# Rotary embedding: the swapped q/k halves from a second projection instead of from two copies

## The chip, the cores and the metric

The kernel runs as one program on one core of a Trainium2 chip. The metric is the device time of one launch in microseconds; lower is better. The engines are TensorE (PE in the profile, its weight loads PEld), VectorE (DVE), ScalarE (ACT), GpSimd (POOL) and SyncE (SP), which here only sends transfers.

## The reference

For x of 2 x 4096 tokens by 512 columns the kernel adds three things: x, an attention branch and an expert branch, both on the layer-normalised x. Cut to the attention's front, which the change touches:

```python
xn = layernorm(x)
c = (xn @ W_to_kv.T) @ W_compress.T              # 64 columns
ch = layernorm(c) * gamma + beta
q = ch @ W_q_comp.T
k, v = split(ch @ W_kv_comp.T)                   # 64 columns each
q = q * cos + rotate_half(q) * sin               # rotate_half(a) = concat(-a[32:], a[:32])
k = k * cos + rotate_half(k) * sin
out = x + causal_attention(q, k, v) @ ... + shared_expert(xn) + top2_of_16_experts(xn)
```

## The kernel before

Three stages follow each other: `prepare` (to about 700 us), `routed` (the 16 experts on gathered rows, to about 1500 us) and `attend`. Only `prepare` changes.

`prepare` works on 16 groups of 512 tokens. Each engine has its own program, written out by hand as functions `step(s, n, q)`: n is the group whose attention front and router are computed, s = n - 1 is the group that goes through the shared expert beside it, and q is the buffer parity. Steps 0 and 1 have their own order (`first_step`, `second_step`); 3 to 12 run in a hardware loop of pairs. Semaphores between engines are the only other thing that sets the order.

fp32 products are made of three fp32r matmuls on a high and a low part, so most tiles come as `_h` and `_l`: ScalarE writes the rounded high part, VectorE the rest. Within a step:

- TensorE computes the gate and up products of group s, the logits, transposes the compressed state (`turn_c`), does the down products, and between them the projection `qkv` (lines 439 and 440): q and k of 512 tokens, transposed, in the PSUM bank `nb`, one 128x512 output from the weights `wqk` and the state `chs`. Then it transposes the next group's normalised rows, four tiles of four transposes (`turn`, line 399), alternating between the PSUM banks `tb[1]` and `tb[0]`. Turns 2 and 3 wait for `xT_l` of the tile two before them. A wait holds up everything behind it.
- `chs` is finished by VectorE (line 721), which does `ew_l` (line 777), the low part of half an expert's weights, shortly before. `ew_l` waits for ScalarE's `ew_h` (line 546), and that for the load of these weights. The weights are sent back to memory split, for `routed`.
- The rows of `wqk` are laid out so that `nb` holds q low half, k low half, q high half, k high half (32 rows each). VectorE multiplies `nb` by the cosines into `t1` (line 746) and signals `straight`. ScalarE then copies the two 64-row halves of `nb`, swapped, into `t2` (lines 571, 572), VectorE multiplies `t2` by the sines (line 753) and adds (line 755) into `qks`. The copy of v (line 749) stands between.
- GpSimd adds the bias to x for group n (`xb`, line 996), four operations that start when VectorE has finished `h_l` of group s (line 765). SyncE's queue is in order too: the load of x for n + 2 waits for `xb`, and behind it stand the stores of the split weights, the loads of the next half expert, four stores of q and k, one of v, and the store of `base`.

Of the kernel before, what the change touches and what calls it, by code (L numbers as in the profile page):

```python
# [25 lines left out]
F32R = mybir.dt.float32r  # L26
# [11 lines left out]
R = C // 2  # L38
# [47 lines left out]
def build(nc, x, w_kv, w_compT, gamma, beta, w_qk, w_vT, w_c2l, w_outT, b_out, routerT,  # L86
# [11 lines left out]
    with ExitStack() as ctx:  # L98
# [19 lines left out]
        prepare(nc, x, w_kv, w_compT, gamma, beta, w_qk, w_vT, b_out, routerT, sh_gate, sh_up,  # L118
# [17 lines left out]
def prepare(nc, x, w_kv, w_compT, gamma, beta, w_qk, w_vT, b_out, routerT, sh_gate, sh_up,  # L136
# [3 lines left out]
    with ctx:  # L140
# [9 lines left out]
        wqk = sb("wqk", [P, 2 * C]); wqkp = [sb(f"wqk_{c}", [P, 2 * C], F32R) for c in "hl"]  # L150
# [54 lines left out]
        swap_done, straight = sem("swap_done"), sem("straight")  # L205
# [15 lines left out]
                 *((wqk[h:h + C, :], w_qk) for h in (0, C)),  # L221
# [46 lines left out]
        def _(sp):  # L268
# [71 lines left out]
            def store_qkv(n, q):  # L340
                sp.wait_ge(qk_done, n + 1)
                sp.wait_ge(v_done, n + 1)
                hold(sp, sp_gate)
                cols = slice(n * GROUP, (n + 1) * GROUP) if isinstance(n, int) else bass.ds(n * GROUP, GROUP)
                for half in range(2):
                    rows_d, at = slice(half * R, half * R + R), 2 * half * R
                    sp.dma_start(q_d[rows_d, cols], qks[q][at:at + R, :]).then_inc(st_qkv[q], 16)
                    sp.dma_start(k_d[rows_d, cols], qks[q][at + R:at + 2 * R, :]).then_inc(st_qkv[q], 16)
                vdst = v_d[n] if isinstance(n, int) else v_d[bass.ds(n, 1)].rearrange("o p c -> (o p) c")
                sp.dma_start(vdst, vs[q][:, :, :].rearrange("p j c -> p (j c)")).then_inc(st_qkv[q], 16)  # L350

            def first_expert():

                for q in range(2):
                    sp.wait_ge(st_qkv[q], 80 * NG // 2)
# [11 lines left out]
        def _(pe):  # L367
# [25 lines left out]
            def turn(n, j):  # L393
                if j == 0:
                    pe.wait_ge(xn_done, n + 1)
                if j > 1:
                    pe.wait_ge(t_ev, 4 * n + j - 1)
                for k in range(KD):
                    mm = pe.transpose(tb[1 - j % 2][:, k * P:(k + 1) * P], xn4[:, j, k * P:(k + 1) * P], ident[:, :])
                mm.then_inc(t_done, 1)  # L400
# [34 lines left out]
            def qkv(n):  # L435
                pe.wait_ge(ch_done, n + 1)
                if known(n, 0):
                    pe.wait_ge(wqk_ev, 2)
                pe.matmul(nb[:, :], wqkp[0][:, :], chs[:, :], start=True, stop=False)
                pe.matmul(nb[:, :], wqkp[1][:, :], chs[:, :], start=False, stop=True).then_inc(qkv_done, 1)  # L440
# [89 lines left out]
        def _(act):  # L530
# [36 lines left out]
            def swapped(n):  # L567

                act.wait_ge(straight, n + 1)
                after(act, qk_done, n)  # L570
                act.copy(t2[0:C, :], nb[C:P, :])
                act.copy(t2[C:P, :], nb[0:C, :]).then_inc(swap_done, 1)

# [5 lines left out]
            def first_step():  # L579
# [9 lines left out]
                swapped(0)  # L589
# [3 lines left out]
            def second_step():  # L593
# [8 lines left out]
                swapped(1)  # L602
# [3 lines left out]
            def step(s, n, q):  # L606
# [22 lines left out]
                if n is not None:  # L629
                    swapped(n)  # L630
# [7 lines left out]
        def _(dve):  # L638
# [146 lines left out]
            def first():  # L785
# [20 lines left out]
                dve.tensor_copy(wqkp[0][:, :], wqk[:, :]).then_inc(wqk_ev, 1)  # L806
                dve.wait_ge(wqk_ev, 1)
                dve.tensor_tensor(wqkp[1][:, :], wqk[:, :], value(wqkp[0][:, :]), ALU.subtract).then_inc(wqk_ev, 1)
# [60 lines left out]
            def first_step():  # L869
# [18 lines left out]
                roped_swapped(0, 0)  # L888
# [5 lines left out]
            def second_step():  # L894
# [14 lines left out]
                for j in range(GT):  # L909
# [4 lines left out]
                    if j == 0:  # L914
                        roped_swapped(1, 1)
# [3 lines left out]
            def step(s, n, q):  # L919
# [45 lines left out]
                for j in range(GT):  # L965
# [4 lines left out]
                    if j == 0 and n is not None:  # L970
                        roped_swapped(n, q)
# [787 lines left out]
def rope_tables():  # L1759
# [6 lines left out]
    cos, sin = cos.T, sin.T  # L1766
    one = np.stack([np.concatenate([cos] * 4), np.concatenate([-sin, -sin, sin, sin])], axis=1)
# [47 lines left out]
```

## Time and profile before

| | us |
|---|---|
| median of 3 runs (lowest, highest) | 1835.32 (1834.62, 1837.1) |
| profiled execution, as timed | 1835.32 |
| its span in the profile | 1833.5 |
| TensorE busy | 1755.7 |
| VectorE busy | 1130.7 |
| ScalarE busy | 771.8 |
| GpSimd busy | 662.4 |

Busy time counts instructions of an engine, not its waits. A row of a timeline gives start, length, engine, line, operation, output and inputs with their sizes, and in brackets the idle time just before and what ended it. The clock is TensorE's granted clock as a share of full speed. Buffer numbers are left out of names, so `t` is `t1` or `t2` and `tb` either bank.

### The profile page before, as it was taken

To read this page: it belongs to the slowest core of one execution; us is meant where nothing else is said; L and a number is where in the kernel's file an instruction comes from. 1 tells how busy PE (TensorE), PEld (TensorE's weight loads), DVE (VectorE), ACT (ScalarE), POOL (GpSimd) and SP (SyncE) were. 2 spreads that over 40 slices of the span, in tenths; PEclk is the share of its full clock that TensorE was granted. 3 is DMA by queue.
4 is the path that set the end of the run, shared out by engine and by line. 5 is a ranking of instruction groups with operands and counts; after the bars stand their busy time and mean duration, and the time that the engine had idled before them with its cause. 6 is when DMAs were issued, how large, how long until landed. Compare 5 with 4: busy or idle time off the path is not lost. (4 is left out here: it accounts for less than half of the span.)

```text
span 1833.5 us, 28152 instructions
## 1 busy us (share of the span) xinstructions
PE 1755.7 (96%) x8477; PEld 1402.1 (76%) x8477; DVE 1130.7 (62%) x2227; ACT 771.8 (42%) x1319; POOL 662.4 (36%) x676
## 2 busy tenths in 40 slices
PE   5699999999999998999999999999999989999998
PEld 3587778787877786778788877778888867777776
DVE  7777667777766653455555555555555436766676
ACT  3232332233222322333333344333333368888885
POOL 2544544545444442343434333433334321011110
PEclk9799999999999999999999999999999999999999
DMA  7667777766677665644544545555445438899896
GB/s 247 244 199 236 219 218 221 240 205 192 206 231 215 200 183 192 198 136 157 184 170 166 177 166 194 178 180 172 165 164 185 153 75 188 205 239 197 208 223 163
DMA packets 149934, 352.52 MB, mean 192 GB/s; under 512 B 20476, under 2 KB 41916, under 8 KB 149824
## 3 DMA queue, kind: packets, MB, share of 16 engines
q1 hardware_dynamic: 97276, 234.52, 39.5%
q0 software_dynamic: 43968, 104.91, 22.5%
q10 hardware_dynamic: 8580, 11.64, 2.3%
q8 instruction: 66, 1.08, 0.2%
q14 instruction: 44, 0.36, 0.1%
HBM read 208.24 MB, written 146.70 MB: 194 GB/s over the span
## 5 line engine op out<-in xcount | busy, mean ns | idle before, releaser
L1486 POOL DMA_INDIRECT expert_rows<-res,ids_all x143 | 150.1, 1050 | 444.8 <-ACT res L1308 435.9
L1427 DVE TENSOR_REDUCE mx<-emb 128x1 f32<-128x512 f32 (+3 forms) x288 | 175.1, 641 | 106.7 <-PE emb L1227 85.2
L70 PE MATMUL egu<-w,rT_0h 128*128 x576 | 186.9, 406 | 1.1 <-DVE rT_0l L1398 1.1
L70 PE MATMUL egu<-w,rT_1h 128*128 x568 | 182.5, 402 | 0.0
L1404 DVE TENSOR_TENSOR eh<-egu,esg 128x256 f32<-128x256 f32 x143 | 60.7, 424 | 183.6 <-ACT esg L1298 183.5
L1682 ACT ACTIVATE ex<-sc 128x1024 f32<-128x1024 f32 (+4 forms) x176 | 144.8, 823 | 55.1 <-PE sc L1627 47.3
L1034 POOL DMA_INDIRECT token_list<-tok,slot x128 | 127.1, 993 | 112.9 <-DVE slot L741 77.0
L1481 POOL DMA_INDIRECT rows<-xn_scratch,rows_all x137 | 132.9, 970 | 48.3 <-issue 43.1
L1298 ACT ACTIVATE esg<-egu 128x256 f32<-128x256 f32 x143 | 55.0, 384 | 204.7 <-PE egu L70 202.0
L1747 POOL DMA_DIRECT2D base<-expert_rows x32 | 41.3, 1527 | 264.8 <-DMA base<-base_scratch 244.2
L996 POOL TENSOR_TENSOR xb<-x,bias 128x512 f32<-128x512 f32 x64 | 88.7, 1417 | 87.9 <-DVE h_l L765 87.9
L70 PEld LDWEIGHTS egu<-w,rT_0h 128*128 128x128 f32 x576 | 104.1, 190 | 21.2 <-issue 1.9
L1626 PE MATMUL sc<-qh,khl 128*128 128x512 f32 (+3 forms) x288 | 112.2, 390 | 7.8 <-ACT pr_2h L1682 2.4
L70 PEld LDWEIGHTS egu<-w,rT_1h 128*128 128x128 f32 x568 | 101.6, 188 | 18.9 <-issue 0.4
L70 PE MATMUL egu<-w,rT_0l 128*128 x288 | 113.8, 395 | 0.0
L70 PE MATMUL egu<-w,rT_1l 128*128 x284 | 111.2, 391 | 0.0
L70 PE MATMUL gb<-wd_h,h_h 128*128 128x512 f32 x256 | 109.1, 426 | 1.1 <-DVE h_l L765 1.1
L1627 PE MATMUL sc<-qlm,kh 128*128 128x512 f32 (+3 forms) x288 | 109.0, 379 | 0.0
L1293 ACT CAST rT_0h<-etb 128x512 fp32r<-128x512 f32 x72 | 42.3, 587 | 157.6 <-PE etb L1186 142.9
L535 ACT ACTIVATE sg<-gb 128x512 f32<-128x512 f32 x64 | 38.2, 597 | 163.4 <-PE gb L70 163.4
L70 PE MATMUL gb<-wd_l,h_h 128*128 128x512 f32 x256 | 103.2, 403 | 0.0
L70 PE MATMUL gb<-wd_h,h_l 128*128 128x512 f32 x256 | 102.4, 400 | 0.0
(283 smaller groups left out, 4563.7 us busy)
## 6 DMA issues: line engine op xcount, KB each, us to landing
w<-expert_parts SPq DMA_DIRECT2D x64, 768.0 KB, 8.5
base<-expert_rows POOLq DMA_DIRECT2D x32, 1024.0 KB, 12.5
expert_parts<-ew_h SPq DMA_DIRECT2D x32, 768.0 KB
expert_parts<-ew_l SPq DMA_DIRECT2D x32, 768.0 KB
x<-x SPq DMA_DIRECT2D x16, 1024.0 KB, 6.2
xn_scratch<-xn SPq DMA_DIRECT2D x16, 1024.0 KB, 8.5
base_scratch<-xb SPq DMA_DIRECT2D x16, 1024.0 KB, 12.2
base<-base_scratch SPq DMA_DIRECT2D x16, 1024.0 KB, 6.5
```

The source lines that it names most:

```text
L70: mm = pe.matmul(dst, w, m, start=(first and i == 0), stop=(last and i == len(terms) - 1))
L996: i = pool.tensor_tensor(xb4[q][:, j, :], x4[q][:, j, :], bias[:, :], ALU.add)
L1034: pool.indirect_dma_start(list_d[:, :], bass.IndirectOffsetOnAxis(ap=slot[q][:, j, c:c + 1], axis=0), tok[q][:, j, c, :], None).then_inc(s ...
L1293: act.copy(rT[t % 2][0][:, :, :], tb[t % 2][:, :].rearrange("p (k t) -> p k t", k=KD)).then_inc(t_hi, 1)
L1298: act.activation(sg[t % 2][:, :], gu[t % 2][:, 0:FE], ACT.Silu).then_inc(sg_done, 1)
L1404: dve.tensor_tensor(h[t % 2][:, :], gu[t % 2][:, FE:2 * FE], sg[t % 2][:, :], ALU.mult).then_inc(h_done, 1)
L1427: dve.tensor_reduce(mx[n % 2][:, j, c:c + 1], mb[g % 2][:, 0:width], AX.X, ALU.max).then_inc(m_red, 1)
L1481: pool.indirect_dma_start(rows[:, t % AHEAD, :], None, xn_d[:, :], bass.IndirectOffsetOnAxis(ap=rows_all[:, t:t + 1], axis=0)).then_inc(ro ...
L1486: pool.indirect_dma_start(parts_d[:, :], bass.IndirectOffsetOnAxis(ap=ids_all[:, t:t + 1], axis=0), res[t % 2][:, :], None, bounds_check=2 ...
L1626: pe.matmul(dst, khl[:, key], qh[k % NQ][:, to:GROUP], start=True, stop=False)
L1627: mm = pe.matmul(dst, kh1[:, key], qlm[k % NQ][:, to:GROUP], start=False, stop=own < 0)
L1682: e = act.activation(dst[:, span(i)], sc[i % 2][:, span(i)], ACT.Exp, scale=SCALE)
```

## The change

A second set of weights, `w_qk_swap`, holds the same columns with the halves of each head swapped. `qkv` runs two more matmuls with it into `tb[0]`. VectorE reads the swapped values from there for the sine product, right behind the cosine product; ScalarE's copies and their two semaphores are gone. Turn 1 of the next group, the next to write `tb[0]`, waits for the sine product (`rope_done`). `qks` now holds q in its first 64 rows and k in the others, so each is one store.

```diff
-        wqk = sb("wqk", [P, 2 * C]); ...
+        wqk = sb("wqk", [P, 2, 2 * C]); ...
-                 *((wqk[h:h + C, :], w_qk) for h in (0, C)),
+                 *((wqk[h:h + C, i, :], w) for h in (0, C) for i, w in enumerate((w_qk, w_qk_swap))),
...
-                for half in range(2):
-                    rows_d, at = slice(half * R, half * R + R), 2 * half * R
-                    sp.dma_start(q_d[rows_d, cols], qks[q][at:at + R, :]).then_inc(st_qkv[q], 16)
-                    sp.dma_start(k_d[rows_d, cols], qks[q][at + R:at + 2 * R, :]).then_inc(st_qkv[q], 16)
+                sp.dma_start(q_d[:, cols], qks[q][0:C, :]).then_inc(st_qkv[q], 16)
+                sp.dma_start(k_d[:, cols], qks[q][C:2 * C, :]).then_inc(st_qkv[q], 16)
...
             def turn(n, j):
+                if j == 1:
+                    after(pe, rope_done, n)
...
-                pe.matmul(nb[:, :], wqkp[0][:, :], chs[:, :], start=True, stop=False)
-                pe.matmul(nb[:, :], wqkp[1][:, :], chs[:, :], start=False, stop=True).then_inc(qkv_done, 1)
+                for i, dst in enumerate((nb, tb[0])):
+                    pe.matmul(dst[:, :], wqkp[0][:, i, :], chs[:, :], start=True, stop=False)
+                    mm = pe.matmul(dst[:, :], wqkp[1][:, i, :], chs[:, :], start=False, stop=True)
+                mm.then_inc(qkv_done, 1)
...
-            def swapped(n):
-                act.wait_ge(straight, n + 1)
-                after(act, qk_done, n)
-                act.copy(t2[0:C, :], nb[C:P, :])
-                act.copy(t2[C:P, :], nb[0:C, :]).then_inc(swap_done, 1)
...
-                dve.tensor_tensor(t1[:, :], nb[:, :], cs[q][:, 0, :], ALU.mult).then_inc(straight, 1)
-                after(dve, st_qkv[q], times(n, q) * 5)
+                dve.tensor_tensor(t1[:, :], nb[:, :], cs[q][:, 0, :], ALU.mult)
+                dve.tensor_tensor(t2[:, :], tb[0][:, :], cs[q][:, 1, :], ALU.mult).then_inc(rope_done, 1)
+                after(dve, st_qkv[q], times(n, q) * 3)
                 dve.wait_ge(cn_done, n + 1)
                 dve.tensor_copy(vs[q][:, :, 0:C - 1], cn[:, :, 0, 0:C - 1]).then_inc(v_done, 1)
-
-            def roped_swapped(n, q):
-                dve.wait_ge(swap_done, n + 1)
-                dve.tensor_tensor(t2[:, :], t2[:, :], cs[q][:, 1, :], ALU.mult).then_inc(rope_done, 1)
                 dve.wait_ge(rope_done, n + 1)
                 dve.tensor_tensor(qks[q][:, :], t1[:, :], t2[:, :], ALU.add).then_inc(qk_done, 1)
```

On TensorE, from the projection to turn 1 of the next group, in group 2. Before:

```order
L439 MATMUL nb<-chs,wqk_h 128x512
L440 MATMUL nb<-chs,wqk_l 128x512
L70 MATMUL gb<-wd_h,h_h 128x512
L70 MATMUL gb<-wd_l,h_h 128x512
L70 MATMUL gb<-wd_h,h_l 128x512
L399 MATMUL tb<-ident,xn 128x128 x4
```

and now (line 397 is the old line 399, 69 the old 70):

```order
L438 MATMUL nb<-chs,wqk_h 128x512
L439 MATMUL nb<-chs,wqk_l 128x512
L438 MATMUL tb<-chs,wqk_h 128x512
L439 MATMUL tb<-chs,wqk_l 128x512
L69 MATMUL gb<-wd_h,h_h 128x512
L69 MATMUL gb<-wd_l,h_h 128x512
L69 MATMUL gb<-wd_h,h_l 128x512
L397 MATMUL tb<-ident,xn 128x128 x4
```

Two matmuls come in behind the two of before; all else keeps its order.

On VectorE, from the end of the projection in the loop's first group. Before:

```order
L746 TENSOR_TENSOR t_61<-nb,cs_59 128x512
L749 COPY vs<-cn 128x4x63
L772 TENSOR_TENSOR xT_0l<-tb,xT_0h 128x4x128
L783 TENSOR_TENSOR xb_0<-gb,xb_0 128x512
L753 TENSOR_TENSOR t_62<-t_62,cs_59 128x512
L755 TENSOR_TENSOR qks_63<-t_61,t_62 128x512
L772 TENSOR_TENSOR xT_0l<-tb,xT_0h 128x4x128
```

and now (758 is the old line 772, 769 the old 783):

```order
L735 TENSOR_TENSOR t_61<-nb,cs_59 128x512
L736 TENSOR_TENSOR t_62<-tb,cs_59 128x512
L739 COPY vs<-cn 128x4x63
L741 TENSOR_TENSOR qks<-t_61,t_62 128x512
L758 TENSOR_TENSOR xT_0l<-tb,xT_0h 128x4x128
L769 TENSOR_TENSOR xb_0<-gb,xb_0 128x512
L758 TENSOR_TENSOR xT_0l<-tb,xT_0h 128x4x128
```

The sine product and the sum moved ahead of the first `xT_l`. In group 0 they moved ahead of `ew_l` as well.

## Rows read from the trace of the kernel before

**Rows 1.** The page: busy us, share of the span and instructions of each engine.

```profile
PE 1755.7 (96%) x8477; PEld 1402.1 (76%) x8477; DVE 1130.7 (62%) x2227; ACT 771.8 (42%) x1319; POOL 662.4 (36%) x676
```

**Rows 2.** Stretches: length, busy us of each engine (instructions), clock, DMA share, GB/s.

```profile
60.00:700.00 640.00, 626.79 (x3023) 498.95 (x3022) 445.86 (x1074) 187.27 (x272) 305.31 (x313) 0.98 0.69 209
```

**Rows 3.** Waits, 60 to 690 us: who for whom, total us, times, longest.

```profile
ACT ew_h L546 <- DMA ew<-down_w: 33.5, 20, 3.9
...
PE nb L439 <- DVE chs L721: 8.1, 6, 3.1
```

**Rows 4.** Timeline of TensorE: the projections with the longest idle time before them.

```profile
210.32 0.50 PE L439 MATMUL nb<-chs,wqk_h 128*128 128x512 f32 x1 [1.55 <-DVE chs L721]
...
252.04 0.50 PE L439 MATMUL nb<-chs,wqk_h 128*128 128x512 f32 x1 [1.56 <-DVE chs L721]
...
534.50 0.50 PE L439 MATMUL nb<-chs,wqk_h 128*128 128x512 f32 x1 [1.07 <-DVE chs L721]
...
578.50 0.80 PE L439 MATMUL nb<-chs,wqk_h 128*128 128x512 f32 x1 [3.11 <-DVE chs L721]
```

**Rows 5.** Timeline of TensorE: a projection without a wait.

```profile
293.83 0.39 PE L439 MATMUL nb<-chs,wqk_h 128*128 128x512 f32 x1
294.06 0.39 PE L440 MATMUL nb<-chs,wqk_l 128*128 128x512 f32 x1
```

**Rows 6.** Timeline, group 1: projection, turn 1, the cosine product.

```profile
87.88 0.63 PE L440 MATMUL nb<-chs,wqk_l 128*128 128x512 f32 x1
88.31 1.06 PE L399 MATMUL tb<-ident,xn 128*128 128x128 f32 x4
...
90.44 1.05 PE L399 MATMUL tb<-ident,xn 128*128 128x128 f32 x4
...
90.50 0.68 DVE L746 TENSOR_TENSOR t<-nb,cs 128x512 f32<-128x512 f32 x1
```

**Rows 7.** Timeline of TensorE, group 10: second projection matmul, turns 1 and 2.

```profile
453.73 0.39 PE L440 MATMUL nb<-chs,wqk_l 128*128 128x512 f32 x1
...
456.05 0.60 PE L399 MATMUL tb<-ident,xn 128*128 128x128 f32 x4
...
459.29 0.60 PE L399 MATMUL tb<-ident,xn 128*128 128x128 f32 x4
```

**Rows 8.** Timeline of VectorE and GpSimd, group 10.

```profile
454.15 0.69 DVE L746 TENSOR_TENSOR t<-nb,cs 128x512 f32<-128x512 f32 x1
454.26 5.53 POOL L996 TENSOR_TENSOR xb<-x,bias 128x512 f32<-128x512 f32 x4 [5.97 <-DVE h_l L765]
454.76 0.93 DVE L749 COPY vs<-cn 128x252 f32<-128x252 f32 x1
...
458.68 1.66 DVE L755 TENSOR_TENSOR qks<-t,t 128x512 f32<-128x512 f32 x1
```

**Rows 9.** Line 755: shortest, median and longest in ns, first and last start.

```profile
L755 DVE TENSOR_TENSOR qks<-t,t x16: 691/1174/1668, 57.8 to 663.7; 128x512 f32<-128x512 f32 x16
```

**Rows 10.** Timeline of SyncE's queue, group 10: the base store.

```profile
468.04 0.39 SPq L338 DMA_DIRECT2D base_scratch<-xb  x1
```

**Rows 11.** Timeline of the start, five engines.

```profile
4.56 1.20 SPq L286 DMA_DIRECT2D wqk<-w_qk  x2
...
12.62 1.97 PE L460 MATMUL nb<-wcT,ht 128*128 128x64 f32 x8 [12.62 <-DMA token<-token_in]
...
15.98 0.23 DVE L806 CAST wqk_h<-wqk 128x128 fp32r<-128x128 f32 x1
...
55.36 1.76 DVE L777 TENSOR_TENSOR ew_l<-ew,ew_h 128x1536 fp32r<-128x1536 f32 x1 [2.60 <-ACT ew_h L546]
...
58.37 1.28 DVE L772 TENSOR_TENSOR xT_1l<-tb,xT_1h 128x512 fp32r<-128x512 f32 x2
...
59.10 1.97 PE L399 MATMUL tb<-ident,xn 128*128 128x128 f32 x8 [7.09 <-DVE xT_1l L772]
```

**Rows 12.** Stretch behind the second wait of rows 4, columns as rows 2.

```profile
253.00:256.50 3.50, 3.50 (x13) 2.78 (x13) 2.24 (x4) 1.75 (x3) 3.50 (x3) 0.52 0.00 0
```

More of the change, by code:

```diff
@@ L37 @@
 C = 64
-R = C // 2
 LAT = 128
@@ L83, in hold, with build @@
     eng.sem_inc(gate, 1)
-def build(nc, x, w_kv, w_compT, gamma, beta, w_qk, w_vT, w_c2l, w_outT, b_out, routerT,
+def build(nc, x, w_kv, w_compT, gamma, beta, w_qk, w_qk_swap, w_vT, w_c2l, w_outT, b_out, routerT,
           gate_w, up_w, down_w, sh_gate, sh_up, sh_down, rope, ident_in, tri_in, route_in, upto_in, token_in, tile_p_in, fold_in, out):
@@ L117, in build @@
         w_in, st_base, stored = sems("w_in", 2), sems("st_base", 2), sems("rstored", 2)
-        prepare(nc, x, w_kv, w_compT, gamma, beta, w_qk, w_vT, b_out, routerT, sh_gate, sh_up,
+        prepare(nc, x, w_kv, w_compT, gamma, beta, w_qk, w_qk_swap, w_vT, b_out, routerT, sh_gate, sh_up,
                 sh_down, rope, ident_in, tri_in, route_in, upto_in, token_in, tile_p_in, q_d, k_d, v_d, base_d, xn_d, list_d,
@@ L133, in build, with prepare @@
         attend(nc, q_d, max_d, base_d, parts_d, out, ident, khl, kh1, vhl, mop, queries, masks, stored, base, base_in, placed)
-def prepare(nc, x, w_kv, w_compT, gamma, beta, w_qk, w_vT, b_out, routerT, sh_gate, sh_up,
+def prepare(nc, x, w_kv, w_compT, gamma, beta, w_qk, w_qk_swap, w_vT, b_out, routerT, sh_gate, sh_up,
             sh_down, rope, ident_in, tri_in, route_in, upto_in, token_in, tile_p_in, q_d, k_d, v_d, base_d, xn_d, list_d,
@@ L149, in prepare @@
         wcT = sb("wcT", [P, C])
-        wqk = sb("wqk", [P, 2 * C]); wqkp = [sb(f"wqk_{c}", [P, 2 * C], F32R) for c in "hl"]
+        wqk = sb("wqk", [P, 2, 2 * C]); wqkp = [sb(f"wqk_{c}", [P, 2, 2 * C], F32R) for c in "hl"]
         gam = sb("gam", [P, 1]); bet = sb("bet", [P, 1]); bias = sb("bias", [P, D])
@@ L204, in prepare @@
         d_done, d_ev = sem("d_done"), sem("d_ev")
-        swap_done, straight = sem("swap_done"), sem("straight")
         scattered = [sem("scattered0"), sem("scattered1")]
@@ L354, in first_expert @@
                 for q in range(2):
-                    sp.wait_ge(st_qkv[q], 80 * NG // 2)
+                    sp.wait_ge(st_qkv[q], 48 * NG // 2)
                 sp.wait_ge(st_xn, 16 * NG)
@@ L588, in first_step @@
                 expert_high(0, 1)
-                swapped(0)
                 for j in range(GT):
@@ L601, in second_step @@
                 expert_high(1, 1)
-                swapped(1)
                 for j in range(GT):
@@ L628, in step @@
                     hidden_high(s, 3)
-                if n is not None:
-                    swapped(n)
                 if n is not None and not known(n, NG - 1):
@@ L805, in first @@
                 dve.wait_ge(wc_ev, 3)
-                dve.tensor_copy(wqkp[0][:, :], wqk[:, :]).then_inc(wqk_ev, 1)
+                dve.tensor_copy(wqkp[0][:, :, :], wqk[:, :, :]).then_inc(wqk_ev, 1)
                 dve.wait_ge(wqk_ev, 1)
-                dve.tensor_tensor(wqkp[1][:, :], wqk[:, :], value(wqkp[0][:, :]), ALU.subtract).then_inc(wqk_ev, 1)
+                dve.tensor_tensor(wqkp[1][:, :, :], wqk[:, :, :], value(wqkp[0][:, :, :]), ALU.subtract).then_inc(wqk_ev, 1)
                 for j in range(GT):
@@ L887, in first_step @@
                 expert_low(0, 1)
-                roped_swapped(0, 0)
                 for j in range(GT):
@@ L913, in second_step @@
                     turned_low(2, 0, j)
-                    if j == 0:
-                        roped_swapped(1, 1)
                     if j == 1:
@@ L969, in step @@
                         added(s, 1 - q, j)
-                    if j == 0 and n is not None:
-                        roped_swapped(n, q)
                     if j == 1 and n is not None:
@@ L1765, in rope_tables @@
     cos, sin = np.cos(angle).astype(f), np.sin(angle).astype(f)
-    cos, sin = cos.T, sin.T
-    one = np.stack([np.concatenate([cos] * 4), np.concatenate([-sin, -sin, sin, sin])], axis=1)
+    cos = np.concatenate([cos, cos], axis=1).T
+    sin = np.concatenate([-sin, sin], axis=1).T
+    one = np.stack([np.concatenate([cos, cos]), np.concatenate([sin, sin])], axis=1)
     seq = one.reshape(2 * C, 2, QB, GROUP).transpose(2, 0, 1, 3)
@@ L1794 @@
     wqT, wkT, wvT = wq.T, wkv[:C].T, wkv[C:].T
+    swap = lambda w: np.concatenate([w[:, C // 2:], w[:, :C // 2]], axis=1)
     ident, tri, route, upto, token, tile_p, fold = shape_tables()
@@ L1798 @@
         "gamma": a["L0_attn_ln_gamma"][:, None], "beta": a["L0_attn_ln_beta"][:, None],
-        "w_qk": np.concatenate([wqT[:, :R], wkT[:, :R], wqT[:, R:], wkT[:, R:]], axis=1),
+        "w_qk": np.concatenate([wqT, wkT], axis=1), "w_qk_swap": np.concatenate([swap(wqT), swap(wkT)], axis=1),
         "w_vT": wvT, "w_c2l": a["L0_attn_W_comp2lat"], "w_outT": a["L0_attn_W_out_res"].T, "b_out": a["L0_attn_b_out_res"],
```

## The prediction

> **What bounds the kernel now.** I read the busy shares first: TensorE is busy for 1755.7 of 1833.5 us [rows 1]. The table of stretches then shows where the change acts: it touches only the preparation, up to about 700 us, where TensorE is busy for 626.8 of 640 us at a clock of 0.98 [rows 2]. ScalarE has 187 us of work there and VectorE 446, so work taken from them is worth nothing by itself; work given to TensorE is paid unless it falls into a wait. The table of waits says which waits there are. Where TensorE stands idle, it is for `chs` from VectorE, just ahead of the q/k projection that the change doubles, and ScalarE spends 33.5 us waiting for expert weights to land, which stand ahead of `chs` on VectorE [rows 3]. The four longest of these idle times are 1.55, 1.56, 1.07 and 3.11 us [rows 4]. So there are two loops of about 40 us per group: TensorE's instruction stream, and expert weights to `chs`. Usually the first is the later one, in a few groups the second. From here on n is the group, 0 to 15, and every time is of one profiled execution, span 1833.5 us, 1835.32 us as timed; the 1.8 us around the span I leave as they are. That execution equals the median shown.
>
> **Two more matmuls in each group.** In a running stream the two projection matmuls start 0.23 us apart (293.83, 294.06) [rows 5]. They are 128x512 like the two that are added, so a group costs 2 x 0.23 = 0.46 us. In group 0 this costs nothing: TensorE waits for the normalised rows of the next group afterwards. Groups 2 to 15: 14 x 0.46 = 6.4 us. In group 1 TensorE runs at the lower of its two clocks, 1.2 GHz (matmul 0.63 us against 0.39, the next thing starts 0.43 us later [rows 6]), so 0.86 us.
>
> **What of that falls into waits.** In the four groups of [rows 4] `chs` comes from the weights' loop. It starts again when VectorE finishes `h_l` and GpSimd can add the bias (the `xb` operations), after which SyncE, having waited for them, sends the x load, the weight stores and the next weight loads. None of this waits for the projection. TensorE arrives 0.46 us later at the next wait, and the wait is 0.46 us shorter: -4 x 0.46 = -1.8 us. Shorter idle entries are left out. Bounds: nothing is hidden (0), or all of groups 2 to 14 (-6.0).
>
> **The new wait of turn 1.** Transposing tile 1 of the next group writes `tb[0]`, which now holds the swapped projection, so it waits until VectorE has multiplied it by the sines. Ahead of it stand, on TensorE, three matmuls, the four transposes of tile 0 and three matmuls. In group 10 the last projection matmul starts at 453.73 and turn 1 at 456.05, 2.32 us later. Its weight load stands 0.23 us before it, one matmul's pitch, so it must be released at +2.09 [rows 7]. VectorE starts the first product at 454.15 (+0.42) and, as the distance to the next row shows, takes an instruction of this kind every 0.61 us [rows 8]. The second product is new in this form (PSUM times SBUF into SBUF), but it is the form and size of the first, 0.69 us: it ends at 0.42 + 0.61 + 0.69 = +1.72. Some 0.1 us for the signal, an estimate, leaves 0.27 us of margin, 0 to 0.1 in groups where TensorE does not start from a wait. I take 0.1 us in a few groups. In group 1 there is no margin: the first product starts at 90.50, the second ends at 91.80, and turn 1, which began at 90.44, could begin at 90.44 + 0.86 = 91.30 [rows 6]. With 0.2 us for signal and weight load it waits 0.7 us. Everything behind it waits too, since TensorE is in order. If it never waited, this term is 0; if VectorE were late by a `v` copy, about 1 us.
>
> **Turn 2 and the shared port.** Turn 2 waits for `xT_l` of tile 0. VectorE now does both products, the copy of v and the sum before it, where the sine product and the sum stood behind it. Two of those, the copy and the sum, run into GpSimd's four `xb` operations. The sum takes 1.66 us in group 10, ending after GpSimd's last operation (454.26 + 5.53 = 459.79, sum 458.68 to 460.34), against 0.69 us as its shortest [rows 8, 9]. So each of the two may wait for one GpSimd operation of some 1.3 us. Shifted by the 0.46 us, GpSimd's first operation starts at about +0.07 relative to the last projection matmul. The copy asks at +1.65, is let in at +2.5 and ends at 2.8; the sum is let in at about +3.8 and ends at 4.5; `xT_l` runs to 5.1. Turn 2 begins at 459.29 - 453.73 = +5.56, its weight load at 5.33 [rows 7]. Margin 0.1 to 0.2 us. Together with turn 1 of the running groups I enter +0.3 us; the bounds are 0 and, if both lose one more operation, the first rival below. GpSimd then ends at the same time as now within 0.1 to 0.5 us, which is why I let the weights' loop stand.
>
> The Trainium skill, page "SBUF — State Buffer", section "SBUF: two separate sides", calls this an exclusive lock: a VectorE instruction with two SBUF inputs and a GpSimd operation that reads SBUF exclude each other for a whole instruction. The trace agrees (1.66 against 0.69 us). By that rule the sine product leaves the lock, since one input now comes from PSUM, and the sum stays in it, now in front of turn 2.
>
> **What goes.** Two ScalarE copies, VectorE's wait for them and the `straight` signal. Nobody on the path waits for them in running groups, since ScalarE is idle most of the time: 0. Two of five stores per group leave SyncE's queue, the bytes stay: 0, since q, k and v are not read before the preparation ends. What they free is that the base store behind them is issued earlier, 1 to 2 us before its 468.04 [rows 10].
>
> **Start.** Two more constant loads stand in SyncE's queue ahead of those that the first matmul waits for. Two such issues take 1.20 us; the first matmul waits until 12.62, and everything after it hangs on it [rows 11]: +1.2. Rounding and splitting 256 instead of 128 columns: 0.23 us for the cast at 128 columns; with a doubling at most 0.5 for the pair, I take +0.3. On the other side, VectorE now finishes its rope work in the idle time ahead of 55.36 and not between `ew_l` and `xT_l`, and ScalarE has no swap in front of its tile copies at 55.36. `xT_l` begins when `ew_l` is through (55.36 + 1.76 = 57.12) and not at 58.37, and turn 2 at 59.10 follows: -1.3 [rows 11]. Bounds of the three together: -0.5 and +2.
>
> **Sum.** 6.4 + 0.86 - 1.8 + 0.7 + 0.3 + 1.5 - 1.3 = +6.7 us. The gathers and the attention start later by that and are unchanged. Span 1840.2, time 1842.0 us.
>
> **Rivals.**
> *A. The port makes turn 2 the bound.* The copy or the sum loses one more GpSimd operation: 1.3 us less the 0.15 of margin is 1.15 us in 13 groups, 15 us: 1857. For it: the sum did lose a whole one [rows 8]. Against it: they lose one each in my count already. 8%.
> *B. The base store collides with the weights.* Issued 1.6 us earlier, it shares the transfer queues with the weight loads still under way. If half of that time is lost to the weights in ten groups, 8 us come on top: 1850. For it: ScalarE waits for just these loads [rows 3]. Against: the order in the queue is unchanged. 10%.
> *C. The weights' loop sets the pace.* Where `chs` releases TensorE everywhere, all 6.0 us of groups 2 to 14 are hidden, 4.2 more than in the sum: 1838. One wait of [rows 4] that gets shorter may also spare a fall to the lower clock: after the 1.56 us the granted clock was 0.52, the 1.2 GHz level, for 3.5 us [rows 12], which costs about half of that, 1.6 us. Then 1836. For it: idle before `chs` is seen in many groups. Against: TensorE is 98% busy. 14%.
> *D. Not slower: the weights land earlier.* Two stores fewer per group leave the queue behind the weight loads. Place: ScalarE's wait for `ew`. If they landed 1.5 us earlier, the four waits would go (7.3 us, of which 1.8 is counted) and two falls of the clock (3.2): 1842.0 - 5.5 - 3.2 = 1833.3. It decides from about 1 us of earlier landing. Against it: the stores stand behind the loads, so they can only have disturbed them by overlap. 8%.
> The Trainium skill, page "DMA: Bandwidth & Descriptors", section "Anatomy of one DMA", gives each transfer about 2 us of fixed cost whatever its size, so by that page two fewer are worth 4 us per group if somebody waits. No row here has anybody waiting for them; it speaks for D alone.
>
> **How the numbers follow.** The forecast, slower by 3 to 10 us (1838.5 to 1845), has 60%; A 8, B 10, C 14, D 8. About 0.2%, 3.7 us, is what a measurement of this kernel can tell from no change. Slower beyond it: most of the forecast (55) and A and B (18), 73%. Within: rest of the forecast, C and a little of D, 20%. Faster: 7%. The range reaches over C below and B above: 1835.5 to 1850; A and most of D stay out.
>
> **What would show it.** Two matmuls more per group into `tb`, 0.23 us apart, and TensorE's busy time up by 6 to 8 us. Idle before the projection about 0.46 us shorter in the groups of [rows 4]. Turn 1 with a wait for the sine product in group 1 and hardly elsewhere. Turn 2 without wait; if it shows one of 1 us in most groups, A is right. First matmul at about 13.8 us. If ScalarE's 33.5 us of waiting for `ew` falls or rises by more than 10 us, D or B. The forecast is wrong if the preparation doesn't end 4 to 10 us later.

## The result and the profile after

| | before, us | changed, us |
|---|---|---|
| median (lowest, highest; runs) | 1834.5 (1832.97, 1837.1; 6) | 1843.73 (1838.6, 1844.86; 6) |
| profiled execution, as timed | 1835.32 | 1834.49 |
| its span | 1833.5 | 1832.7 |

The changed kernel takes 1.0053 of the time of before, 95% interval 1.0036 to 1.0069: slower, by 9.7 us in the middle of the interval, where I had forecast 6.7. But its profiled execution was a quick one, 4 us under the fastest of its timed runs. On its trace alone the change would look free, so I use it for the order of things and compare a second trace of each kernel. These are from two other chips, on which before takes 1850.24 us (the changed kernel's) and 1850.69 us (before's); times are compared as ratios on one chip only.

The first trace of the changed kernel answers the busy times of [rows 1] and the stretch of [rows 2]:

```profile
PE 1759.1 (96%) x8509; PEld 1406.6 (77%) x8509; DVE 1135.1 (62%) x2227; ACT 752.7 (41%) x1287; POOL 660.1 (36%) x676
...
60.00:700.00 640.00, 630.54 (x3055) 503.76 (x3054) 450.34 (x1077) 169.49 (x242) 303.58 (x313) 0.99 0.68 210
```

32 more matmuls, and ScalarE has 18 us less to do there. Group 10 in its timeline, against [rows 7, 8]:

```profile
456.56 0.39 PE L439 MATMUL nb<-chs,wqk_l 128*128 128x512 f32 x1
456.79 0.39 PE L438 MATMUL tb<-chs,wqk_h 128*128 128x512 f32 x1
457.02 0.39 PE L439 MATMUL tb<-chs,wqk_l 128*128 128x512 f32 x1
457.09 5.54 POOL L977 TENSOR_TENSOR xb<-x,bias 128x512 f32<-128x512 f32 x4 [5.91 <-DVE h_l L751]
457.45 0.69 DVE L735 TENSOR_TENSOR t<-nb,cs 128x512 f32<-128x512 f32 x1 [0.56 <-PE tb L439]
...
458.06 0.68 DVE L736 TENSOR_TENSOR t<-tb,cs 128x512 f32<-128x512 f32 x1
458.66 1.13 DVE L739 COPY vs<-cn 128x252 f32<-128x252 f32 x1
459.09 0.60 PE L397 MATMUL tb<-ident,xn 128*128 128x128 f32 x4
459.71 1.77 DVE L741 TENSOR_TENSOR qks<-t,t 128x512 f32<-128x512 f32 x1
461.40 0.68 DVE L758 TENSOR_TENSOR xT_1l<-tb,xT_1h 128x512 fp32r<-128x512 f32 x1
...
462.33 0.60 PE L397 MATMUL tb<-ident,xn 128*128 128x128 f32 x4
```

The added matmuls start 0.23 us apart, turn 1 (459.09) has no bracket and so no wait, nor has turn 2 (462.33). The sum takes 1.77 us. This part went as worked out. The second trace of the changed kernel, its page and its table of waits (60 to 690 us):

```profile
span 1854.0 us, 28109 instructions
...
PE 1765.4 (95%) x8509; PEld 1408.7 (76%) x8509; DVE 1137.0 (61%) x2227; ACT 753.5 (41%) x1287; POOL 657.5 (35%) x676
...
ACT ew_h L546 <- DMA ew<-down_w: 57.5, 23, 7.3
...
PE nb L438 <- DVE chs L710: 9.5, 10, 2.4
...
PE tb L397 <- DVE t L736: 0.3, 1, 0.3
```

and the second trace of before:

```profile
span 1851.0 us, 28152 instructions
...
PE 1758.0 (95%) x8477; PEld 1402.1 (76%) x8477; DVE 1132.2 (61%) x2227; ACT 771.9 (42%) x1319; POOL 656.2 (35%) x676
...
ACT ew_h L546 <- DMA ew<-down_w: 53.0, 25, 5.6
...
PE nb L439 <- DVE chs L721: 17.8, 9, 5.2
```

TensorE is 7.4 us busier, and its idle time for `chs` is 8.3 us shorter: the matmuls stand where it would have waited. Yet the span is 3.0 us longer. Where that arises is seen at `chs` of group 2 and of group 15, changed:

```profile
127.74 0.69 DVE L710 TENSOR_TENSOR chs<-t,chs 64x512 fp32r<-64x512 f32 x1
...
674.47 0.69 DVE L710 TENSOR_TENSOR chs<-t,chs 64x512 fp32r<-64x512 f32 x1
```

and before:

```profile
128.53 0.69 DVE L721 TENSOR_TENSOR chs<-t,chs 64x512 fp32r<-64x512 f32 x1
...
672.26 0.69 DVE L721 TENSOR_TENSOR chs<-t,chs 64x512 fp32r<-64x512 f32 x1
```

In group 2 the changed kernel is 0.8 us ahead; from there to group 15 it needs 546.7 us against 543.7. A pair of traces does not prove 3 us, since executions differ by as much (the first pair has 527.9 against 530.1) and these two come from different chips; it says where to look. In the first pair TensorE's idle time for `chs` is shorter, too, against 8.1 us in [rows 3]:

```profile
PE nb L438 <- DVE chs L710: 1.0, 2, 0.6
```

### The profile page after: what moved, and what is told of

It is laid out like the page before. It is cut to its first block and busy times, and to the rows that moved or that the text cites. A ratio compares the mean times of both kernels' runs of the same rounds, so it can differ in the third digit from the quotient of the medians.

```text
span 1832.7 us, 28109 instructions
## 1 busy us (share of the span) xinstructions
PE 1759.1 (96%) x8509; PEld 1406.6 (77%) x8509; DVE 1135.1 (62%) x2227; ACT 752.7 (41%) x1287; POOL 660.1 (36%) x676
## 5 line engine op out<-in xcount | busy, mean ns | idle before, releaser
L69 PEld LDWEIGHTS egu<-w,rT_1h 128*128 128x128 f32 x568 | 101.7, 188 | 19.8 <-issue 0.6
```

Source lines behind the costliest of these rows:

```text
L69: mm = pe.matmul(dst, w, m, start=(first and i == 0), stop=(last and i == len(terms) - 1))
```

## The experiments

All ratios are against before on the same chip, with 95% intervals. The first batch asks which part of the change costs the time.

**The changed kernel again, with a second trace.** No edit.

> The changed kernel once more. Its six timed runs had a median of 1843.7 us, but the one execution that was profiled took 1834.5 us, so its trace may be an untypical one. If the extra time is TensorE's two added matmuls alone, every execution pays it and this one's preparation ends 6 us later or more; the quick execution then had luck in its waits. If the extra time comes from the loop of expert weights (weights landing later, TensorE idle before the projection), this trace shows more idle time before the projection than the quick one, and the time scatters by several us from run to run. Ratio to before: 1.004 to 1.006 by either.

Measured: 1.0036 (1.0022 to 1.0049). Slower again, on another chip; the interval overlaps the first. The trace shows more idle time before the projection than the quick one (9.5 us against 1.0) and more waiting for the weights (57.5 against 32.4), the sign that was named for the loop of weights. The kernel before shows as much of a difference between its own two traces (17.8 against 8.1, 53.0 against 33.5), so the sign does not tell the change from the chip.

**Before, with the projection done twice.** The two matmuls are issued twice into `nb`, nothing else:

```diff
-                pe.matmul(nb[:, :], wqkp[0][:, :], chs[:, :], start=True, stop=False)
-                pe.matmul(nb[:, :], wqkp[1][:, :], chs[:, :], start=False, stop=True).then_inc(qkv_done, 1)
+                for i in range(2):
+                    pe.matmul(nb[:, :], wqkp[0][:, :], chs[:, :], start=True, stop=False)
+                    mm = pe.matmul(nb[:, :], wqkp[1][:, :], chs[:, :], start=False, stop=True)
+                mm.then_inc(qkv_done, 1)
```

> The kernel of before, whose projection into nb is simply done twice with the same weights (same result): two more 128x512 matmuls per group and nothing else, no new wait, no other order on VectorE, the same stores. Theory 1, TensorE's stream pays: 14 x 0.46 us plus group 1, less what falls into waits, +4 to +7 us, ratio 1.002 to 1.004, that is most of what the change costs. Theory 2, the cost is in the weights' loop, which the other parts of the change lengthened: the doubling falls into the waits for chs, 0 to +3 us, ratio under 1.002.

Measured: 0.9993 (0.998 to 1.0005), which is -1.3 us (-3.7 to +0.9). With 32 more matmuls in the same place the kernel is not measurably slower. The largest term of my sum was 6.4 us, 4.6 after what falls into waits, and both lie outside the interval. But the doubling moves something else as well. VectorE starts on `nb` later (1.60 us after `chs`, 0.95 in the second trace of before) and its sum no longer meets GpSimd (median 0.69 us, as when free), and the x load is issued 6.21 us after `chs` instead of 6.51 (means of groups 2 to 12). So this run shows the net of the matmuls and of a slightly shorter loop of weights, not the matmuls alone. A pair without this difference comes in the third batch.

**The changed kernel with four stores of q and k again**, of 32 rows each, as before the change:

```diff
-                sp.dma_start(q_d[:, cols], qks[q][0:C, :]).then_inc(st_qkv[q], 16)
-                sp.dma_start(k_d[:, cols], qks[q][C:2 * C, :]).then_inc(st_qkv[q], 16)
+                for lo in (0, C // 2):
+                    half = slice(lo, lo + C // 2)
+                    sp.dma_start(q_d[half, cols], qks[q][half, :]).then_inc(st_qkv[q], 16)
+                    sp.dma_start(k_d[half, cols], qks[q][C + lo:C + lo + C // 2, :]).then_inc(st_qkv[q], 16)
```

> The changed kernel with q and k stored in four pieces of 32 rows again, as before, so that the base store and the rope load are issued as late as they were. Theory 1: no difference to the changed kernel, +9 us against before. Theory 2 in the form of rival B (the base store, issued earlier, disturbs the landing of the expert weights): 3 to 8 us faster than the changed kernel, and the first half of the weights lands about 11 us after the issue of its last load instead of about 12.3.

Measured: 1.0032 (1.0015 to 1.0049), as without the edit. In the trace the base store is issued 14.9 us after `chs` instead of 13.95 (means of groups 2 to 12), the first half of the weights lands 0.4 us sooner and the second 1.0 us later. The number of stores and the moment of the base store make no difference that shows.

**The changed kernel with one constant load per half**: `w_qk` and `w_qk_swap` side by side in one array, so that SyncE's queue has no more issues than before:

```diff
-                 *((wqk[h:h + C, i, :], w) for h in (0, C) for i, w in enumerate((w_qk, w_qk_swap))),
+                 *((wqk[h:h + C, :, :], w_qk.rearrange("p (i c) -> p i c", i=2)) for h in (0, C)),
```

> The changed kernel with the two sets of projection weights in one array, so that as many constant loads stand ahead of the first matmul as before. By the prediction the start gets 1.2 us shorter (first matmul at about 12.6 instead of 13.9 us) and the whole kernel 1.2 us faster than the changed one. If the start is absorbed later, no difference in time.

Measured: 1.0015 (1.0001 to 1.003). The trace has `chs` of group 2 at 126.52 instead of 127.74. The ratios differ by 3.9 us, with overlapping intervals; the trace shows 1.2 us, the two issues, and no cause for more.

What is left is the new place of the sine product, the copy of v and the sum. The second batch moves them.

**The copy of v and the sum behind the third `xT_l`**, in the changed kernel. GpSimd's `xb` operations then have the port to themselves:

```diff
                 dve.tensor_tensor(t2[:, :], tb[0][:, :], cs[q][:, 1, :], ALU.mult).then_inc(rope_done, 1)
+
+            def summed(n, q):
                 after(dve, st_qkv[q], times(n, q) * 3)
...
+                    if j == 2 and n is not None:
+                        summed(n, q)
```

> The changed kernel with the copy of v and the sum moved on VectorE from just behind the products to behind the third xT_l, when GpSimd's four xb operations have ended. Theory P: the load of x is issued 0.5 us earlier after chs (6.2 instead of 6.7), each of some 12 groups gets 0.5 us shorter, 5 to 7 us less than the changed kernel, about the time of before. Theory S: the scatters start even earlier (the sum, 1.8 us, no longer stands before them), so no gain or a loss of a few us.

Measured: 1.0076 (1.0063 to 1.0089), the opposite of what the port's theory wanted, though its first half came true. Group 6 of this kernel:

```profile
303.17 0.69 DVE L710 TENSOR_TENSOR chs<-t,chs 64x512 fp32r<-64x512 f32 x1
304.79 5.04 POOL L984 TENSOR_TENSOR xb<-x,bias 128x512 f32<-128x512 f32 x4 [6.71 <-DVE h_l L753]
310.17 0.37 SPq L274 DMA_DIRECT2D x<-x  x1
311.74 1.08 POOL L1022 DMA_INDIRECT token_list<-tok,slot  x1 [1.91 <-DVE slot L730]
313.51 0.56 SPq L302 DMA_DIRECT2D ew<-down_w  x1
326.66 1.48 ACT L546 CAST ew_h<-ew 128x1536 fp32r<-128x1536 f32 x1 [3.87 <-DMA ew<-down_w]
```

of the changed kernel:

```profile
298.45 0.69 DVE L710 TENSOR_TENSOR chs<-t,chs 64x512 fp32r<-64x512 f32 x1
300.07 5.55 POOL L977 TENSOR_TENSOR xb<-x,bias 128x512 f32<-128x512 f32 x4 [6.45 <-DVE h_l L751]
302.68 1.78 DVE L741 TENSOR_TENSOR qks<-t,t 128x512 f32<-128x512 f32 x1
304.38 0.68 DVE L758 TENSOR_TENSOR xT_1l<-tb,xT_1h 128x512 fp32r<-128x512 f32 x1
305.96 0.37 SPq L274 DMA_DIRECT2D x<-x  x1
309.15 1.08 POOL L1015 DMA_INDIRECT token_list<-tok,slot  x1 [3.53 <-DVE slot L730]
309.44 0.93 SPq L302 DMA_DIRECT2D ew<-down_w  x1
321.17 1.48 ACT L546 CAST ew_h<-ew 128x1536 fp32r<-128x1536 f32 x1 [3.09 <-DMA ew<-down_w]
```

and of before:

```profile
296.31 0.69 DVE L721 TENSOR_TENSOR chs<-t,chs 64x512 fp32r<-64x512 f32 x1
300.37 0.69 DVE L772 TENSOR_TENSOR xT_1l<-tb,xT_1h 128x512 fp32r<-128x512 f32 x1 [1.01 <-ACT xT_1h L576]
303.68 0.38 SPq L276 DMA_DIRECT2D x<-x  x1
306.86 0.50 SPq L304 DMA_DIRECT2D ew<-down_w  x1
307.52 1.08 POOL L1034 DMA_INDIRECT token_list<-tok,slot  x1 [4.06 <-DVE slot L741]
318.07 1.48 ACT L546 CAST ew_h<-ew 128x1536 fp32r<-128x1536 f32 x1 [2.32 <-DMA ew<-down_w]
```

From the end of `chs` in group 6, the x load comes at 6.31 us with the sum late, 6.82 in the changed kernel and 6.68 before. So the `xb` operations do end earlier when VectorE leaves them alone. But `token_list`, the first of GpSimd's eight small scatters, comes at 7.88, 10.01 and 10.52, and from the issue of the last weight load to `ew_h` it is 13.15, 11.73 and 11.21 us. In these three traces, the earlier the scatters, the later the weights. The scatters wait for VectorE's `slot`. Before the change VectorE stood idle for 1.01 us ahead of the first `xT_l`, because ScalarE did its swap copies before its part of that tile; in the changed kernel the rope work fills this time, so `slot` and the scatters come sooner. With the sum late, the copy of v and the sum no longer stand ahead of `slot` at all. Here is the rate of the transfers in two stretches, 12 to 14 and 14 to 16 us after `chs` (last column, GB/s; the others as in [rows 2]), with the sum late:

```profile
315.90:317.90 2.00, 2.00 (x11) 1.65 (x10) 0.00 (x0) 0.00 (x0) 1.66 (x2) 1.00 1.03 426
317.90:319.90 2.00, 2.00 (x11) 1.48 (x10) 0.00 (x0) 0.45 (x1) 1.39 (x3) 1.00 1.14 209
```

in the changed kernel, with the two microseconds after:

```profile
311.10:313.10 2.00, 2.00 (x10) 1.66 (x9) 0.00 (x0) 0.00 (x0) 1.39 (x3) 1.00 1.05 428
313.10:315.10 2.00, 2.00 (x10) 1.53 (x9) 0.00 (x0) 0.36 (x1) 1.70 (x2) 1.00 1.02 405
315.10:317.10 2.00, 2.00 (x10) 1.28 (x9) 1.04 (x2) 0.86 (x2) 1.39 (x3) 1.00 1.11 209
```

and before, 14 to 16, 16 to 18 and 18 to 20 us:

```profile
311.00:313.00 2.00, 2.00 (x10) 1.49 (x9) 0.00 (x0) 0.59 (x1) 1.39 (x3) 1.00 1.01 402
313.00:315.00 2.00, 2.00 (x10) 1.33 (x9) 1.27 (x2) 0.63 (x2) 1.63 (x2) 1.00 1.14 311
315.00:317.00 2.00, 2.00 (x11) 1.60 (x10) 2.00 (x5) 0.58 (x1) 1.45 (x2) 1.00 1.16 320
```

The DMA share stays at 1 or above while the rate falls, some 6 us after the first scatter: from 426 and 405 to 209 GB/s in the first two kernels, from 402 to 311 before. One would guess that the scatters occupy the transfer engines. The queues say otherwise. With the sum late, the same two stretches by queue (packets, MB, share of the time of 16 engines; q1 holds SyncE's transfers, q0 GpSimd's scatters), first 315.9 to 317.9:

```profile
q1 hardware_dynamic: 159, 0.85, 101.7%
q0 software_dynamic: 32, 0.00, 1.2%
```

and 317.9 to 319.9:

```profile
q1 hardware_dynamic: 68, 0.42, 112.7%
q0 software_dynamic: 27, 0.00, 1.6%
```

The scatters' own packets take 1.6% of the time. It is SyncE's packets that take twice as long: 0.85 MB in 101.7% of the time, then 0.42 MB in 112.7%. What makes them slow is not shown.

**Before, with the sine product, the copy of v and the sum behind the third `xT_l`.** No matmul and no constant load is added:

```diff
+
+            def roped_swapped(n, q):
                 after(dve, st_qkv[q], times(n, q) * 5)
...
-
-            def roped_swapped(n, q):
...
-                    if j == 0 and n is not None:
-                        roped_swapped(n, q)
...
+                    if j == 2 and n is not None:
+                        roped_swapped(n, q)
```

> The kernel before with v copy, sine product and sum moved behind the third xT_l, clear of GpSimd's xb operations. Theory P: the load of x at 6.1 to 6.2 us after chs in every group instead of 6.1 to 6.7, so 0.3 us per group, 2 to 5 us faster than before. Theory S: the scatters start earlier here, too, so slower than before by some us.

Measured: 1.0034 (1.0022 to 1.0046). By this move alone the kernel before gets about as slow as the changed one. Its first scatter comes at 8.35 us after `chs` and the weights take 13.19 (means, below). Two things keep this from being the proof for the change. It is another move: it brings the scatters forward by 2.3 us (10.61 to 8.35), four times the 0.6 of the change, and costs no more. And its trace does not lose the time where the scatters were measured: from group 2 to 15 it needs 544.0 us, before 543.7 on the same chip. The 2.9 us that it is behind stand ahead of group 2 (`chs` at 131.47 against 128.53).

**The slots behind the third `xT_l`**, in the changed kernel; the scatters start later, the rope work stays:

```diff
-                    if j == 1 and n is not None:
+                    if j == 2 and n is not None:
```

> The changed kernel with VectorE's computation of the slots, which releases GpSimd's scatters, one tile later in its order (behind the third added tile instead of the second), which starts the scatters some 3 us later. Theory S: the first half of the weights lands 1 to 2 us sooner after its issue (11 to 12 instead of 13 us) and the kernel is 5 us or more faster than the changed one. Theory P: no change beyond 2 us, the load of x still at 6.7 us after chs.

Measured: 1.0027 (1.0013 to 1.004). The first half of the weights lands in 11.69 us instead of the 13.15 of the changed kernel on the other chip, as expected, but the second half needs 9.0 instead of 7.27, and the gain in time is within the intervals. From group 2 to 15 the trace needs 550.0 us, not less than the 546.7. A miss for the theory of the scatters alone.

**Before again, for its trace.** No edit.

> The kernel before, for a trace on this chip, where it takes some 1850 us. Theory P (GpSimd's xb operations end later after the change, because the v copy and the sum of VectorE fall between them): the load of x is issued here 6.2 to 6.5 us after chs, against 6.7 in the changed kernel. Theory S (the scatters into the token list start earlier in the changed kernel and disturb the expert weights on their way): the weights of the first half land here about 11 us after the issue of their last load, against 13.1.

Measured: 1.0008 (0.9995 to 1.0021), what the method gives for no change.

The third batch takes both: the copy of v and the sum behind the second `xT_l`, the slots behind the third. First in the changed kernel:

> The changed kernel with v copy and sum behind the second added tile (GpSimd's xb operations are over) and the slots behind the third. The load of x should be issued 6.2 us after chs (6.7 in the changed kernel) and the first scatter not earlier than before the change (10.6 or later). Theory L, the weights' loop is the cost, and two things lengthen it, GpSimd ending 0.5 us later and the scatters starting 0.6 us earlier: both gone, so 5 to 7 us faster than the changed kernel, ratio to before 1.000 to 1.001. Rival, the two added matmuls are the cost after all: ratio stays 1.003 or more.

Measured: 1.0018 (1.0005 to 1.003). From its waits, 60 to 690 us:

```profile
ACT ew_h L546 <- DMA ew<-down_w: 11.4, 9, 3.3
```

11.4 us of waiting for the weights instead of 57.5, on another chip, though.

**The same with one constant load per half.**

> The same with the two weight sets in one constant load: 1.2 us less than after_both_late at the start. By theory L the ratio to before is 0.999 to 1.0005, the best form of this change.

Measured: 1.0009 (0.9996 to 1.0022). No longer to be told from before, with the added matmuls in place. Each remedy alone gave 1.0015 (the loads) and 1.0018 (the moves); these three intervals overlap each other. All three lie below the interval of the first result (1.0036 to 1.0069); against the second (1.0022 to 1.0049) the first two overlap it and the last just touches it.

**Before with the same two moves.**

> The kernel before with v copy, sine product and sum behind the second added tile and the slots behind the third: the load of x at 6.2 us after chs instead of 6.5, the first scatter at 10.6 us or later. Theory L: 0 to 4 us faster than before. If only the start of the scatters counts, no difference.

Measured: 0.9998 (0.9987 to 1.001). Before has nothing to gain from them, and no version measurably beats it. This run also gives the cleaner test of the matmuls. It and the version above, with one constant load per half, issue the x load and the first scatter nearly alike (6.17 and 11.29 us after `chs` here, 6.19 and 11.47 there), and only the latter has the added matmuls (and not ScalarE's two copies). From group 2 to 15 they need 522.3 and 521.7 us, and their ratios are 0.9998 and 1.0009, some 2 us apart, with overlapping intervals. So the matmuls cost little in the loop; a cost of 1 or 2 us is not excluded.

**The changed kernel without the added matmuls.** The swapped projection is left out, so q and k get other numbers:

```diff
-                for i, dst in enumerate((nb, tb[0])):
+                for i, dst in enumerate((nb,)):
```

> The changed kernel without the two added matmuls: the projection is done once, the swapped one is left out (the sine product reads what lies in the bank, so q and k are other numbers), and everything else, waits, order, loads and stores, is that of the changed kernel. Theory L: the matmuls cost next to nothing, so the ratio to before stays at 1.002 to 1.004. Rival, TensorE's stream is the cost: 5 to 7 us faster than the changed kernel, ratio 1.000.

Measured: 1.012 (1.0097 to 1.0143), a miss for both theories. The changed kernel is slower without the work that I had held for its cost than it ever was with it, though on this chip it was not run itself. VectorE now starts some 0.5 us earlier on its rope work (0.93 us after `chs` instead of 1.40), and the first scatter comes at 8.88 us after `chs` instead of 9.99. From group 2 to 15 its trace has 536.2 us, where the traces of both late on that chip have 521.2 and 522.3, so two thirds of the 22 us are there. Its first half of the weights lands in 12.72 us, no later than in the changed kernel. Why it loses so much, more than before with the rope late, whose scatters start sooner still, is open, and it is the strongest objection to any account by the scatters.

Means over groups 2 to 12, in us; A to D are the four chips, and each trace is one execution. First scatter is counted from the end of `chs`; the landings from the issue of a half's last load to `ew_h`, in those of the 11 groups where ScalarE waited for it by more than 0.3 us (their number in brackets where it is under 6); group 2 to 15 is from `chs` to `chs`.

| | chip | first scatter | 1st half lands | 2nd half lands | group 2 to 15 | ratio |
|---|---|---|---|---|---|---|
| before, first trace | A | 10.61 | 10.98 | 8.04 | 530.1 | 1 |
| changed, first trace | A | 10.23 | 12.33 | 6.76 (1) | 527.9 | 1.0053 |
| before, twice the projection | B | 10.80 | 11.15 | 8.96 | 540.0 | 0.9993 |
| changed | B | 9.99 | 13.15 | 7.27 | 546.7 | 1.0036 |
| changed, four stores | B | 10.0 | 12.76 | 8.3 | 550.0 | 1.0032 |
| changed, one load | B | 10.0 | 12.7 | 8.18 | 543.6 | 1.0015 |
| before | C | 10.61 | 11.58 | 8.79 | 543.7 | 1.0008 |
| before, rope late | C | 8.35 | 13.19 | 7.78 | 544.0 | 1.0034 |
| changed, slots late | C | 11.81 | 11.69 | 9.0 | 550.0 | 1.0027 |
| changed, sum late | C | 7.87 | 14.7 | 7.93 (3) | 554.8 | 1.0076 |
| before, both late | D | 11.29 | 10.32 (4) | 10.64 (3) | 522.3 | 0.9998 |
| changed, both late | D | 11.39 | 11.37 (3) | 8.15 (3) | 521.2 | 1.0018 |
| changed, both late, one load | D | 11.47 | 10.41 (2) | 10.24 (2) | 521.7 | 1.0009 |
| changed, one projection | D | 8.88 | 12.72 | 7.6 (3) | 536.2 | 1.012 |

First scatter and first half go together on all four chips: scatters from 10.6 us on, weights in 10.3 to 11.7; scatters at 10.2 or less, 12.3 to 14.7. No run on a single chip moves the scatters alone, though. The second half often gives back a part. The time does not follow: slots late has early weights and 550.0 us, rope late has late weights and 544.0, as much as before. Only sum late has, against before on the same chip, both later weights and a slower loop. So the scatters do not account for the cost by themselves.

## Why the forecast came out, and where its steps did not

*Two more matmuls, 6.4 us, less 1.8 in waits.* This is the step that failed. The pitch of 0.23 us was right, and the group's stream on TensorE did get 0.46 us longer, but the sum charged it to the time in all but four groups. Done twice in the kernel before, the projection costs -1.3 us (-3.7 to +0.9), with a slightly shorter loop of weights in it; in the two kernels with both moves, whose x loads and scatters start alike, group 2 to 15 takes 521.7 us with the matmuls and 522.3 without. I had read "TensorE 98% busy" as "TensorE bounds". The waits of [rows 3] said something else: a loop of weights and transfers returns to `chs`, and what TensorE does beside it is taken from its next wait. Its idle time for `chs` is 7.1 us shorter in the first pair and 8.3 in the second. Rival C had this mechanism, at 14%.

*"GpSimd then ends at the same time as now within 0.1 to 0.5 us, which is why I let the weights' loop stand."* The number was right (x load 6.74 us after `chs` against 6.51, means) and the conclusion wrong. I looked only at that part of the loop. The router's slots stand behind the first `xT_l` on VectorE, where the wait for ScalarE is gone, so the scatters went forward by 0.4 to 0.6 us (10.61 to 10.23 and 9.99), and that I had not put into the sum at all. Shown: the place of the rope work on VectorE changes the time without any matmul added, by 1.0034 in the kernel before; moving the copy and the sum out of the port's way, and so the scatters further forward, makes the changed kernel worse, 1.0076; with both moves and one load no difference to before can be measured. Not shown: that the scatters, half a microsecond earlier, are what the change pays for, and how the loss divides between the port, the scatters and the start, since each remedy alone left intervals that overlap.

*Rival B* had the right place (transfers that collide with the weights while ScalarE waits for them) and the wrong transfer: four stores moved the base store by 1 us and nothing followed in the time. The ones that go together with late weights come from GpSimd's queue, not from SyncE's. ScalarE's wait rose by 4.5 us in the second pair and fell by 1.1 in the first, both under the 10 us I had asked for as a sign.

*Rival D* falls: with two stores fewer the weights landed later. The section of the Trainium skill that I cited for it, page "DMA: Bandwidth & Descriptors", section "Anatomy of one DMA", describes transfers that GpSimd issues, and these stores are issued by SyncE, so it was no ground for a price here. As the forecast said, nobody waits for them.

*Turns 1 and 2.* Right for the running groups: from group 1 on, turn 1 waits for the sine product only in group 1, 0.34 us at 91.09 instead of the 0.7 that I had entered. In group 0 it waits 2.06 us (54.46), which I had not foreseen; it costs nothing there, since turn 2 waits behind it for `xT_l`. Turn 2 has no wait in the rows above. Counted from the last matmul's start (457.02), the copy of v ends at +2.77, the sum at +4.46 and `xT_l` at +5.06, forecast 2.8, 4.5 and 5.1. Rival A falls.

*Shared port.* The sum takes 1.777 us as median in the changed kernel, 1.656 in the trace of before from a like chip, against 0.69 when free; with the sum late it took 0.67 us (312.83), and `xb` 5.04 instead of 5.55 us. This is the lock that I cited from the Trainium skill, page "SBUF — State Buffer", section "SBUF: two separate sides". The traces agree in both directions: each side loses time to the other. Giving GpSimd its half microsecond back won nothing by itself; the scatters came sooner with it.

*Start.* The first matmul waits until 14.02 instead of 12.75 (second traces; 13.8 was forecast), and with one load per half `chs` of group 2 comes 1.2 us earlier: right. The sum had the changed kernel 1.8 us behind by group 2 (0.86 + 0.7 + 1.5 - 1.3); the first pair of traces has it 1.7 behind (130.0 against 128.3), the second 0.8 ahead. In group 0 turn 2 starts at 59.69 us in the first trace of the changed kernel and at 58.00 in the second, against 59.10 and 59.09 before. It follows `ew_l`, and that the landing of the weights, whose `ew_h` starts at 55.77 and 54.07: the gain of 1.3 us that I had entered hangs on a landing that differs by more than that between two executions.

*The sign that I had named.* I had called the forecast wrong if the preparation did not end 4 to 10 us later. It did not, in either pair: `chs` of group 15 starts at 657.27 us against 657.65 before in the first, and 2.2 us later than before in the second. TensorE's busy time rose by 3.4 and 7.4 us, 6 to 8 forecast. The first trace is that of the quick execution; no trace shows where the timed runs lose their 9.7 us.

So the direction was right, the size near (6.7 us against 9.7, interval 6.6 to 12.7), and the main reason wrong: 4.6 us charged for matmuls that cost little or nothing stood in for a cost elsewhere, in the order of VectorE's work and what hangs on it, which I had ruled out. That the total came out near is luck.

## What to carry to other kernels

An engine that is 98% busy need not be the bound: look what its few waits end on and follow that loop, since work added beside it can be nearly free where a reordering inside it is not. When an instruction moves in an engine's program, list everything behind it down to the next transfer that this starts, on every queue, GpSimd's scatters included, and ask what that transfer will meet. And test the dearest term by itself, by doing it twice in the old kernel, as here, where it overturned the account; then read in the trace what else the doubling has moved.

## What the runs showed of the hardware

- Large transfers are slow while GpSimd's small scatters are under way, though the scatters hardly use the transfer engines. With the sum late, the rate drops from 426 to 209 GB/s about 6 us after the first of eight is issued, at a DMA share above 1, of which the scatters' queue takes 1.6%; SyncE's packets take twice the time per byte. On one chip the first half of the weights lands in 14.7 us with the first scatter at 7.87 us after `chs`, in 11.6 with it at 10.61. That the scatters cause it is inferred from the order in time; why they should was not tried.
- Two matmuls of 128x512 added per group to a stream with 98% busy share cost little or nothing: 0.9993 (0.998 to 1.0005) in the kernel before, and 521.7 against 522.3 us from group 2 to 15 with both moves.
- VectorE's sum of two SBUF tiles takes 1.78 us beside GpSimd's additions and 0.67 us clear of them; four of these take 5.54 us beside the sum and 5.04 clear of it.
